# Both layer norms' linear part as a 256-column TensorE product, squares summed by ScalarE, powers on GpSimd

## What is computed

```python
hidden = gelu(x @ down_W.T + down_b)                       # 32 features
hidden = hidden @ expert_W[d].T + expert_b[d] + domain_emb[d]
s = hidden @ up_W.T + up_b + x                             # the sum
x1 = (s - mean(s)) * rsqrt(var(s) + 1e-5) * ln_gamma + ln_beta
```

```python
h = (x1 - mean(x1)) * rsqrt(var(x1) + 1e-5) * ln_g + ln_b  # over the 128 features
h = (h - mean_t(h)) * rsqrt(var_t(h) + 1e-8)               # over the 256 tokens of a sample
gamma, beta = split(style(subject_id)); gamma = softplus(gamma) + 1e-8
h = h * gamma + beta
gates = top2(softmax(h @ router_w)), made to sum to 1
out = x1 + sum over 8 experts of gate_e * (relu(h @ W1_e + b1_e) @ W2_e + b2_e)   # 128 -> 512 -> 128
```

## Time and profile before

| | us |
|---|---|
| median of three runs | 125.94 |
| the three runs | 126.09, 122.81, 125.94 |
| the profiled execution | 122.93 |
| its span, first to last instruction | 121.1 |
| outside the span | 1.83 |
| TensorE busy | 114.2 |
| VectorE busy | 93.1 |
| ScalarE busy | 86.6 |
| GpSimd busy | 54.3 |
| mean granted TensorE clock | 0.972 |

### The profile page before, as it was taken

One profiled execution on the slowest core, in us unless ns is written; L12 is line 12 of the kernel. 1 busy time (PEld: TensorE's weight loads), 2 busy tenths in 40 slices (PEclk: granted clock), 3 DMA queues, 4 the chain that ended last, 5 costly groups with the idle time before them and its releaser, 6 DMA issues.

```text
span 121.1 us, 1653 instructions
## 1 busy us (share of the span) xinstructions
PE 114.2 (94%) x515; PEld 86.5 (71%) x515; DVE 93.1 (77%) x238; ACT 86.6 (71%) x147; POOL 54.3 (45%) x75
## 2 busy tenths in 40 slices
PE   6999889999859999999999999999999999999990
PEld 2557533888548888788888888888888888888780
DVE  4756999999996699895867777685959577776871
ACT  2157596589789996978778787878787876878300
POOL 5200986420594001100089997948577940312300
PEclk9999756999999999999999999999999999999999
DMA  1998599990000005065999100000000000000006
GB/s 64 374 221 341 138 438 449 349 349 16 0 3 0 0 0 173 8 184 133 345 431 425 54 0 0 5 0 0 0 0 0 0 0 0 5 0 0 0 0 173
DMA packets 4328, 14.17 MB, mean 117 GB/s; under 512 B 544, under 2 KB 1888, under 8 KB 4064
## 3 DMA queue, kind: packets, MB, share of 16 engines
q1 hardware_dynamic: 2880, 9.67, 22.4%
q0 software_dynamic: 1008, 3.67, 8.9%
q10 hardware_dynamic: 432, 0.73, 1.7%
HBM read 13.52 MB, written 0.56 MB: 116 GB/s over the span
## 4 chain that ended last, share of the span: by engine, by line
PE 73%; DVE 21%; issue 2%; ACT 1%
PE bank L577 21%; PE bank L578 20%; PE bank L616 11%; PE bank L596 11%; PE bank L621 4%; DVE hid_low L990 3%; DVE x L887 2%; DVE h_full L969 2%; DVE stats L894 1%; DVE h_low L975 1%; DVE z L931 1%; PE bank L548 1%; DVE bank L879 1%; DVE t_stats L915 1%; DVE stats L846 1%
## 5 line engine op out<-in xcount | busy, mean ns | idle before, releaser
L491 ACT ACTIVATE hid_high<-bank,early_sb 128x512 fp32r<-128x512 f32 x64 | 44.3, 692 | 16.1 <-PE bank L596 16.0
L990 DVE TENSOR_TENSOR hid_low<-bank,hid_high 128x512 fp32r<-128x512 f32 x51 | 34.6, 687 | 18.8 <-ACT bank L494 18.3
L494 ACT ACTIVATE bank<-bank,early_sb 128x512 f32<-128x512 f32 x51 | 33.5, 658 | 0.0
L301 POOL TENSOR_TENSOR w_low<-w_raw,w_high 128x256 fp32r<-128x256 f32 x32 | 23.0, 743 | 12.1 <-ACT w_high L479 6.1
L616 PE MATMUL bank<-hid_low,w_high 128*128 128x512 f32 x64 | 25.6, 399 | 1.5 <-DVE hid_low L990 1.3
L577 PE MATMUL bank<-h_high,w_low 128*128 128x512 f32 x64 | 25.6, 400 | 0.7 <-ACT h_high L473 0.7
L577 PE MATMUL bank<-hid_high,w_low 128*128 128x512 f32 x64 | 25.7, 402 | 0.0
L578 PE MATMUL bank<-h_high,w_high 128*128 128x512 f32 x64 | 25.3, 396 | 0.0
L596 PE MATMUL bank<-h_low,w_high 128*128 128x512 f32 x64 | 25.1, 394 | 0.0
L578 PE MATMUL bank<-hid_high,w_high 128*128 128x512 f32 x64 | 25.0, 391 | 0.0
L311 POOL TENSOR_TENSOR y_sum<-y_sum,y_part 128x512 f32<-128x512 f32 x9 | 11.6, 1291 | 19.0 <-DVE y_part L1010 16.9
(11 more groups left out here) (136 smaller groups left out, 110.3 us busy)
## 6 DMA issues: line engine op xcount, KB each, us to landing
w_high<-w_all_dram POOLq DMA_DIRECT2D x7, 512.0 KB, 6.9
w_raw<-w_all_dram SPq DMA_DIRECT2D x1, 3072.0 KB, 10.9
gate_all<-gate_scratch SPq DMA_DIRECT2D x4, 512.0 KB, 5.5
gate_all<-gate_scratch SPq DMA_DIRECT2D x1, 2048.0 KB, 11.4
w_raw<-w_all_dram SPq DMA_DIRECT2D x2, 512.0 KB, 7.8
style_sb<-style_dram SPq DMA_DIRECT2D x1, 324.0 KB, 4.8
tables_sb<-tables_dram ACTq DMA_DIRECT2D x1, 272.0 KB, 3.0
xT_sb<-xT_dram SPq DMA_DIRECT2D x1, 256.0 KB, 3.6
```

Of the source, the lines that this page charges most:

```text
L301: nc.gpsimd.tensor_tensor(w_low[:, e % W_RING, quarter(q)], w_raw[:, e, quarter(q)], w_high[:, e % W_RING, quarter(q)].bitcast(F32), ALU.s ...
L491: ac(hid_high[:, slot, :], hid_ps[slot][:, :], ACT.Relu, bias=bias).then_inc(relu_steps, 1)
L494: ac(hid_ps[slot][:, :], hid_ps[slot][:, :], ACT.Relu, bias=bias).then_inc(relu_steps, 1)
L990: v.tensor_tensor(low, ps, high.bitcast(F32), ALU.subtract).then_inc(low_vector, 1)
```

## The change

- The centring, the gain ln_gamma and the covariance with ln_beta are linear in the sum s. They are put into a matrix `moments` of 128 x 256: 127 columns whose squares sum to the centred energy of s, one column (`K_DIFF`) for the covariance, and 128 columns (`K_SHARE` on) that give centred s times gain. `residual` and `up` now move 256 columns. The matrix is built in the front: GpSimd makes `centring`, `gain_rows` and `up_b_rows` from two new loads of single columns (`ln0_cols`, `up_b_col`), TensorE multiplies (`build_gain`, `up_bias`, `transpose_up`, `build_up`), and ScalarE copies out three times.
- ScalarE sums the squares (`energies`), VectorE takes statistics only of the 128 gained columns. The variance of x1 follows from small operations (`sum_var`, `token_var`); centre and the statistics of x1 go.
- x1 is kept times its standard deviation (`x1_std`, `shifted`), and GpSimd's `adapter_out` makes x1 later, between split_lows(3) and load_high(6). z tiles are shared: VectorE the even, GpSimd the odd of half 0; GpSimd all of half 1.
- Roots of half 1 and the feature roots are powers on GpSimd (`ALU.pow`). ScalarE no longer reloads the sqrt table behind softplus, nor exp at unit 8.
- Expert 0's rounded weights come by DMA (`load_high(0)`). GpSimd's list is reordered: split_lows(1, (0, 1)) now stands behind normalise(2).
- h of each half is shared otherwise: `round_h` on VectorE for the odd sample, h_full of the odd sample on ScalarE.
- WARM_LOAD is 6, WARM_BUILD 2, WARM_NORM (6, 2, 2). ids are loaded through ScalarE's queue, the style load is cut in two.

```diff
-WARM_LOAD, WARM_NORM = 10, (5, 6, 3, 2)
+WARM_LOAD, WARM_BUILD, WARM_NORM = 6, 2, (6, 2, 2)
 # SP
-            sp.dma_start(ids_i[:, :], ids).then_inc(ids_loaded, 16)
+            sp.dma_start(ln0_cols[:, :], ln_row.rearrange("a b d -> d (a b)"), allow_slow_non_contiguous=True
+                         ).then_inc(ln0_cols_loaded, 16)
             sp.dma_start(xT_sb[:, 0:HN], xT[:, 0:HN]).then_inc(x_loaded[0], 16)
+            sp.dma_start(up_b_col[:, :], early[A:A + 1, up_b_at:up_b_at + D].rearrange("a d -> d a"),
+                         allow_slow_non_contiguous=True).then_inc(up_b_loaded, 16)
 # GpSimd, the list
             load_high(1)
-            split_lows(0)
-            normalise(0)
-            split_lows(1, (0, 1))
+            normalise(0, (1,))
+            normalise(1, (1,))
+            split_lows(0, (0, 1))
+            feature_rstd(0)
+            split_lows(0, (2, 3))
             load_high(2)
             load_high(3)
-            pool.wait_ge(affine_ready, HB)
+            sum_std(2)
+            sum_std(3)
+            token_rstd(2)
+            normalise(2, range(T))
+            split_lows(1, (0, 1))
+            token_rstd(3)
+            normalise(3, range(T))
             split_lows(1, (2, 3))
             load_high(4)
             load_high(5)
-            normalise(2)
+            feature_rstd(1)
             pool.wait_ge(affine_ready, B)
             split_lows(2)
             split_lows(3)
+            adapter_out()
 # ScalarE
+            act.wait_ge(gain_in_psum, 1)
+            ac(moments[:, K_DIFF:2 * D], gain_ps, ACT.Copy).then_inc(gain_ready, 1)
+            act.wait_ge(up_T_in_psum, 1)
+            ac(up_T[:, :], up_T_ps, ACT.Copy).then_inc(up_T_ready, 1)
+            act.wait_ge(up_moments_in_psum, 1)
+            ac(up_moments[:, :], up_moments_ps, ACT.Copy).then_inc(up_moments_ready, 1)
...
+            energies(0)
+            sum_std(0)
             act.wait_ge(style_in_psum, 4)
             ac(sty1_T[:, :], sty1_ps, ACT.Relu, bias=col(C_SB1, SC)).then_inc(style_ready, 1)
+            energies(1)
+            token_std(0)
+            sum_std(1)
...
+            token_std(1)
             softplus()
+            energies(2)
+            energies(3)
             round_h(0)
+            for q in range(6):
+                relu_unit(q)
             round_h(1)
 # TensorE
-                mm(sum_ps[b][:, t, :], xT_sb[:, (b * T + t) * P:(b * T + t + 1) * P], ident[:, :],
-                   start=(t == 0), stop=False, skip_group_check=True)
+                mm(sum_ps[b * T + t], xT_sb[:, (b * T + t) * P:(b * T + t + 1) * P], moments[:, :],
+                   start=(b < HB or t == 0), stop=False, skip_group_check=True)
...
+            for q in range(3):
                 first_highs(q)
             pe.wait_ge(h_ready, 1)
+            for q in range(3):
                 first_low(q)
-            first_product(2)
             first_product(3)
+            second_product(0)
+            first_product(4)
             pe.wait_ge(sum_taken, T * HB + T)
             router(0)
-            second_product(0)
-            first_product(4)
             second_product(1, between=lambda: transpose_z(2))
 # VectorE, the list
+            take_adapter(0)
+            shift_moments()
+            take_adapter(1)
             style_step(0)
             sum_stats(0)
+            sum_mv(0)
+            style_step(1)
+            sum_var(0)
+            token_var(0)
+            shifted(0)
+            style_step(2)
             sum_stats(1)
+            sum_mv(1)
+            token_rstd(0)
+            normalise(0, 0)
+            sum_var(1)
+            token_var(1)
+            shifted(1)
+            token_rstd(1)
+            normalise(1, 0)
             minus_abs()
             sum_stats(2)
+            sum_mv(2)
+            feature_stats(0)
             sum_stats(3)
+            feature_stats(1)
+            feature_mv(0)
             softplus(0)
             softplus(1)
             softplus(2)
+            feature_affine(0)
+            round_h(0)
             full_h(0)
             low_h(0)
+            sum_var(2)
+            sum_mv(3)
+            sum_var(3)
             split_unit(0)
+            token_var(2)
+            shifted(2)
             split_unit(1)
+            token_var(3)
+            shifted(3)
```

591 lines of the change are left out of this document (319 added, 272 removed).

## The result

| | before | after |
|---|---|---|
| median | 125.13 us (4 runs, 122.81 to 126.09) | 133.53 us (4 runs, 132.95 to 137.41) |
| ratio | | 1.079, 95% interval 1.061 to 1.097 |
| profiled execution, its span | 122.93, 121.1 us | 133.78, 132.0 us |
| first product (S) | 21.24 | 26.64 |
| first_product(9) | 36.23 | 47.08 |

The prediction was 128.8, its range 124.7 to 131.0: the sign is right, the size is not. Ratios with an interval leave out the longer executions of either kernel, and medians are over all; where the two tell different things of one kernel (experiments 14 and 21), it is for that reason.

A forecast was written before the change was run, and what follows sets the result against it. The first product's start and the time from it to first_product(9) were taken to decide: 24.2 + 16.8 + 84.9 = 125.9, with 1.83 outside 127.7, plus 1.1 for the clock 128.8 us; range 124.7 to 131.0.

The forecast's parts named there:

- a stand of TensorE before unit 4: After second_product(0), TensorE waits 2.7 us for expert 1's low quarter, made on GpSimd behind normalise(2).
- The new chain before the gelus: In the front, from ln0_cols landing through the matrix build and gelus to the table load; roots can begin at 11.0.
- rival (c): In the front, single-element loads land as late as the ln row did: 129.2 to 131.5 us, chance 0.10.
- it isn't the columns that set their pace: In the front, the 256 moving columns of residual and up were priced at nothing.
- affine 0.7, with GpSimd's quarters beside it: On VectorE before the first product, the affine takes 0.7 us; no term for a collision with GpSimd.
- chain T to S, VectorE never waits for TensorE: From when the roots can begin (11.0) to the first product, small steps added without such waits: 13.2 us.
- from unit 4 to first_low(8): Behind the stand in the product phase, TensorE has 8.0 us of work with nothing late.
- power 0.2: On GpSimd, each power replacing a root takes 0.2 us, priced by the row nearest in size.
- GpSimd's z tile 0.44: In half 1's norms, a 128x128 z tile on GpSimd takes 0.44 us, two 0.87.
- ScalarE's hold: In the front, ScalarE waits 2.3 us behind the style relu before energies(1).
- rival (d): TensorE's clock falls in the 2.7 us stand: +1.5 to 3.1, so 129.2 to 130.8 us, chance 0.17.
- The 1.1 us for the clock: Added to the summed time for a low TensorE clock: 1.1 us, a third of the runs' scatter.

The follow-up runs named there:

- experiments 14 and 21: Kernel before with seven filler products around first_highs(8)'s wait, run in two sessions: 122.98 us, ratio 0.994; then 122.97 us, ratio 0.982.
- e6: Kernel before with every product of residual and up issued twice, into the unused half of its bank: 127.93 us, ratio 1.031.
- e4: Kernel before with 40 more fp32 products at its end, to price records: about 0.12 us with 128 moving columns, 0.22 with 256, 0.43 with 512.
- e16: Kernel after with four of GpSimd's low quarters behind a wait for half 0's affine, ahead of half 1's powers: 132.59 us, ratio 1.057.
- e15: Kernel before with small VectorE operations added at its end: three products 0.29 us with GpSimd idle, 1.34 beside its tensor_tensor, 0.58 beside its tensor_scalar.
- e5: Kernel before with 20 GpSimd instructions added behind its last block, to price forms: multiply then add 0.44 us, subtract then multiply 0.79, two-column power 0.70.
- e9: Kernel after with GpSimd's first six low quarters before z's odd tiles, and z tiles as add then multiply: 131.16 us, ratio 1.057.
- e17: Kernel after with four low quarters behind half 0's affine on GpSimd, and z tiles as add then multiply: 131.33 us, ratio 1.053.
- e2: Kernel after with 12 filler products between second_product(0) and first_product(4): 134.6 us, ratio 1.088.
- e1: Kernel after with expert 1's first two low quarters made ahead of load_high(2) instead of behind normalise(2): 134.45 us, ratio 1.079.
- e20: Kernel after with four quarters behind half 0's h_low, add-then-multiply z tiles, style relu behind energies(1), second adapter behind its up product: 130.59 us, ratio 1.039.
- e7: Kernel after with GpSimd's first six low quarters made before the odd tiles of z: 133.85 us, ratio 1.069.

## Why the prediction was right and wrong

**Right.** The tail: 84.9 us from first_product(9), to a tenth. The order's two effects: a later first product and a stand of TensorE before unit 4 behind normalise(2), with its releaser and its length (3.02 for 2.7). The new chain before the gelus: table load over at 11.6, forecast 11.0. That single-element loads are not much later than others: rival (c) fell, GpSimd used ln0_cols at 3.07 us and up_b_col at 5.60, though TensorE then waited 1.11 us for what GpSimd made of the second. Two of the sums are off by 0.05 and 0.1 (7.75 for 7.70, T + 1.85 for T + 1.95), which decides nothing.

**Wrong.** Each term is set beside what the runs gave.

| step of the prediction | it had | measured | from |
|---|---|---|---|
| "it isn't the columns that set their pace", priced at nothing | 0 | +2.0 on S | e6, e4 |
| affine 0.7, with GpSimd's quarters beside it | no term | +0.9 on S by the rows, 0.8 by e16's S | 0.57 + 0.65 for 2 x 0.16; e16, e15 |
| chain T to S, VectorE never waits for TensorE | 0 | waits 1.89 for the second adapter matrix, 1.20 for a style product | profile after |
| from unit 4 to first_low(8) "8.0 with nothing late" | 8.0 | 11.85 | profile after |
| power 0.2 | 0.2 | 0.70 | e5 |
| GpSimd's z tile 0.44 | 0.44 | 0.79; 1.2 to 1.3 on the stretch | e5, e9, e17 |

The first was argued from one row: four records of 256 columns for down took 0.63, less than four of 128 for residual. e4 shows a 256-column record at 0.22 with 32 loaded columns as with 128, and four of them, end to end, at 1.03. Why down's are quicker was not tried; in the code its two samples of a half are given different positions in the array (`tile_position`), so that they may overlap. A pace read from products that may overlap is no pace for products that may not. The upper bound stood in the prediction, 3 us with 2 of them hidden; what is hidden turned out to be little.

The second was not in the sum as a kind of cost at all. The kernel before holds GpSimd back with a wait for the affine, so its rows show no collision. The page of the Trainium skill named above (SBUF — State Buffer, Who interferes with whom) speaks for it. The diff takes that wait out, and that should have been a rival with a price.

The third goes with the first: with 256 columns TensorE's list runs late, and VectorE's list, which the prediction added up without a wait, stands behind it. So the style relu ended at T + 6.1 and token_std(0) at T + 6.7 (17.71 and 18.31, with T = 11.6), forecast at T + 3.9 and T + 5.05; from T to S it was 15.0 for 13.2. Of the 2.3 us that the prediction counted as spent on ScalarE's hold, VectorE's rows show 0.77 as a wait. The first two costs cover S and a little more: 3.0 + 2.0 + 0.9 = 5.9, and S moved by 5.4. The 0.5 between is put down to nothing; the 2.0 were measured in the kernel before, and need not be the same to a tenth in the kernel after.

Behind S, the stand is 3.0 and then two things end together. TensorE runs at the low level from 34.75 to 41.15, 6.4 us for what takes about half of it at the full one, so some 3 us: rival (d), whose price (1.5 to 3.1) was right and whose chance (0.17) was too low. Beside it half 1's norms, with powers of 0.7 and tiles of 0.79, are so late that without the low clock h_low comes 1.03 late (e2). Taking one away shows the other (e1 and e2 leave 18.3 and 18.2); only order and form together bring the stretch to 15.6 (e9), from 20.4 and against 15.0 before.

The sum is then 127.7 + 2.0 + 0.9 - 0.5 + (5.45 - 1.8) = 133.8, and the profiled execution took 133.78. It closes because 0.5 and 5.45 are differences read from that execution; only 2.0 and 0.9 come from elsewhere. The largest step that failed is the stretch: 3.65 us more than forecast, the low clock (some 3 us) and half 1's late norms covering each other. The 1.1 us for the clock that the prediction added stood for the scatter of the kernel before; in the kernel after it has its own place, and is larger.

With every order that was found, and the better form, 5.5 us of the 8.4 remain (e20). 2.0 are the columns. The rest is not divided by a run: it is what the prediction had in S (a chain of small operations in place of centre and statistics), the powers, and the low clock behind first_low(8) (1.6 in e20's profile, where the span less first_product(9) is 86.5).

## What to carry over

A matrix product used to carry linear algebra is priced by its moving columns when nothing overlaps it; take the pace from products that wait for one another. Before taking out a wait between GpSimd and VectorE, ask which small operations of VectorE it kept apart from GpSimd's tensor_tensor: each can be held for as long as those run, and moving them only chooses which chain is hit. A kernel whose runs scatter may have one short stall in which TensorE's clock falls; fillers in that stall, in time that was lost anyway, gave 2% here, more than any part of the change.

## What the hardware showed that was not expected

- VectorE's h_low took 2.33 us for 0.42 (e16): it was issued as the second of four quarters began and ended with the last, while in e15 and e7 small operations got in after each quarter. Why is open.
- A GpSimd power costs by the column: 0.70, 5.4 and 20.8 us for 2, 32 and 128. Subtract then multiply is 0.79 on a 128x128 tile where add then multiply is 0.44.
- ScalarE's square with accumulation is followed by a record of its own, 0.20 us each time.
- TensorE's fp32 records of the front ran at half pace until 10 to 13 us in three profiles, though the granted clock of that stretch is shown as 1.00 in two of them (0.72 in e17): the column doesn't tell all of its pace.
- The table load of 1.28 us began as the last gelu ended (8.37 + 1.92 = 10.29, load at 10.31), and the first square at 11.60: so here too no drain is to be seen beside it.
